# One order of steps in an expert layer: 24 shared steps, all 39 routed tiles in a row, then 20 shared steps

## The chip, the cores and the metric

The kernel runs on one core of a Trainium2 chip. The time is that of one launch on the device, in microseconds (us), median of several runs. The core has TensorE (PE, matrix products; PEld is its weight load), VectorE (DVE), ScalarE (ACT), GpSimd (POOL) and SyncE (SP, which here only starts DMAs), 16 DMA engines, an on-chip memory of 128 partitions, and PSUM banks into which PE writes.

## What is computed

Two layers act on 2048 tokens of 512 features, each an attention-like part and a feed-forward part, each part with layer norm and a residual. The change is in the last part, a mixture of experts:

```python
shared = jnp.einsum('ti,hi->th', jax.nn.silu(x @ sh_gate_w.T) * (x @ sh_up_w.T), sh_down_w)   # I_SH = 1408
probs = softmax(x @ router_weight.T);  top_v, top_i = top_k(probs, 2)                         # 8 experts
for e in range(E):
    gu = x @ gate_up_proj[e].T
    gate, up = (gu[:, :I_MOE], gu[:, I_MOE:])                                                 # I_MOE = 352
    cur = jax.nn.silu(gate) * up @ down_proj[e].T
    out = out + cur * combine[:, e:e + 1]
out = out + jax.nn.sigmoid(x @ shared_gate_w.T) * shared
```

## The kernel before

`build` calls four phases; the last is `experts_phase`. All matrix products are in float32 split in two: every operand has a high part (`_hi`, an ACT copy to a shorter format) and a low part (`_lo`, the difference, made on DVE), and each product is three matmuls (hi·hi, hi·lo, lo·hi).

Each token goes to its two best experts only. POOL scatters the token rows to a DRAM buffer `moe_xs` sorted by expert and padded to tiles of 128 rows; there are always `RT_TILES` = 39 tiles, and the expert that owns a tile is read from the table `owner` at run time.

The work is a list made by `expert_items()`, which each engine walks in the same order, doing its own share of every item:

- **("S", n)**, a shared step, n from 0 to 43: block n // 11 of 512 tokens, chunk n % 11 of 128 hidden columns. PE does gate and up into `moe_ps_g`, `moe_ps_u` (24 matmuls of 512 columns, `shared_gu`) and the down product of step n-1 into the four banks `moe_acc` (12 matmuls, `shared_down`). ACT and DVE split the weights of the next step (`sgu_split`, `sd_split`), DVE multiplies (`s_mul`, tile `moe_hs`), both split the product. It loads 512 KB and 256 KB of weights.
- **("R", i)**, a routed tile. PE does gate and up of tile i (`routed_gu`, 24 matmuls of 352 columns), turns the input of tile i+1 (`turn_xs`), does the down product of tile i-1 (`routed_down`, 9 matmuls) and turns the product of tile i (`turn_h`). ACT and DVE split the weights that come: a "pair" (half of gate and up, 128x1408, `pair_split`) twice, and the down weights (128x1536, `rd_split`), then `xs_split`, `hT_split`, `r_mul` (tile `moe_hr`), `rows`. SP loads 2 x 704 KB and 768 KB of weights into `y`, 256 KB of rows from `moe_xs`, and stores 256 KB of rows to `moe_rows`.
- **("C", m)**, the combine of token tile m: POOL gathers its two rows per token, DVE mixes and takes the statistics (`mix`, `stats`, `shift`), ACT normalises (`norm`), POOL adds the residual. **("F", m)** finishes the last four tiles.

Routed weights have short rings: three pair buffers (the load of pair p waits for the DVE split of pair p-3, `pair_lo`), two down buffers, two input buffers. SP starts its DMAs strictly in the order of its program: in tile n the input of tile n+2, pair 2n+4, the store of tile n-2, the down weights of tile n+1, pair 2n+5. DVE's order in tile n is `hT_split(n-1)`, `rd_split(n-1)`, `pair_split(2n+2)`, `r_mul(n)`, `xs_split(n+1)`, `pair_split(2n+3)`. `turn_h(n)`, the last thing that PE does in a tile, waits for `xs_split(n+1)`.

The list before, in short (`PRE_SHARED` = 12): S0 to S10, the loads of the first tiles (R-1), S11, R0, R1, S12, R2, R3, S13, ..., R36, R37, S30, R38, S31, R39, S32, R40, S33, S34, C0, C1, S35, C2, C3, ..., S39, C10, C11, S40, C12, S41, C13, S42, C14, S43, C15, S44 (the last down product), F12 to F16. R39 and R40 hold only what is left of tiles 38 and 37.

Of the kernel before, what the change touches and what calls it, by code (L numbers as in the profile page):

```python
# [1101 lines left out]
DK = 3  # L1102
LAST = I_MOE - 2 * P
NL = 10
PRE_SHARED = 12
CMB = TPB * (NB - 1)


def expert_items():

    items = [("S", n) for n in range(PRE_SHARED - 1)] + [("R", -1), ("S", PRE_SHARED - 1)]
    n = PRE_SHARED
    for i in range(RT_TILES):
        items.append(("R", i))
        if i % 2:
            items.append(("S", n))
            n += 1
    items += [("S", n), ("R", RT_TILES), ("S", n + 1), ("R", RT_TILES + 1)]
    n += 2
    todo, left = list(range(NT)), N_SH - n  # L1120
    for k in range(left):
        items.append(("S", n + k))
        if k:
            share = -(-len(todo) // (left - k))
            items += [("C", m) for m in todo[:share]]
            todo = todo[share:]
    return items + [("S", N_SH)] + [("F", m) for m in range(CMB, NT)] + [("F", NT)]


def experts_phase(nc, io, keep):  # L1130
# [9 lines left out]
    with ExitStack() as ctx:  # L1140
# [59 lines left out]
        acc = [ps(f"acc{t}") for t in range(TPB)]  # L1200
        io_xs, io_rows = io["moe_xs"], io["moe_rows"]
        items = expert_items()

        def free_gu(eng, k):
# [1150 lines left out]
```

## Time and profile before

| | us |
|---|---|
| median of 3 runs | 2231.64 (2224.86 to 2236.63) |
| the profiled execution | 2235.23 |
| its span, first to last instruction | 2233.5 |
| expert phase, first product of the router to the end | 1515.4 to 2233.5 |
| PE busy | 2008.1 (90%) |
| DVE / ACT / POOL busy | 1478.4 / 1180.8 / 712.8 |
| moved by DMA | 244.97 MB, mean 110 GB/s |

A time line of an engine has, in each row, the start, the duration, the line of the kernel, the tile written and those read, and in square brackets how long the engine had been idle and whose work ended that. Times are from the start of the span. Matmuls overlap, so the step from one start to the next tells PE's pace, not the duration. The "granted clock" (PEclk) is 1.00 at 2.4 GHz and 0.50 at 1.2 GHz.

### The profile page before, as it was taken

Reading aid. Unit: us, or ns where it says so; the run is one execution under the profiler, and the core shown is the slowest. Engines: PE = TensorE matmul, PEld = TensorE weight load, DVE = VectorE, ACT = ScalarE, POOL = GpSimd, SP = SyncE. Lnnn points to the kernel's source line nnn. Section 1 sums busy time; section 2 is a strip of 40 time slices with the busy share of each in tenths; the row PEclk is TensorE's granted clock in tenths of the full one; section 3 lists DMA queues with packets and bytes.
Section 4 is the critical chain, followed back from the end, with each engine's and each line's share of the span. In section 5 each row is a group of like instructions: output and inputs, shape, how many; then the busy total and the mean of one; then the engine's idle time right before and its main releaser. Section 6 shows DMA issues by size and latency. Waiting matters only on the chain. (4 is left out here: it accounts for less than half of the span.)

```text
span 2233.5 us, 32625 instructions
## 1 busy us (share of the span) xinstructions
PE 2008.1 (90%) x10142; PEld 1682.8 (75%) x10142; DVE 1478.4 (66%) x3466; ACT 1180.8 (53%) x2944; POOL 712.8 (32%) x1013
## 2 busy tenths in 40 slices
PE   6885999966999999999999999868689999999976
PEld 4664778744888888888888888757578888888754
DVE  6556655774667767676667677885247777767475
ACT  4663222234666666666666666643246666766332
POOL 0123000143555555555555555640500000000263
PEclk9887999977999999999999999978899999999998
DMA  4143111128000000000000000123568888887463
GB/s 186 43 160 127 42 30 34 38 95 289 16 20 11 20 10 20 10 20 10 20 10 20 10 1 2 62 71 100 209 222 285 298 283 290 293 286 265 144 217 122
DMA packets 78765, 244.97 MB, mean 110 GB/s; under 512 B 9729, under 2 KB 10369, under 8 KB 76577
## 3 DMA queue, kind: packets, MB, share of 16 engines
q1 hardware_dynamic: 73488, 226.46, 29.5%
q0 software_dynamic: 5120, 16.78, 2.2%
q8 instruction: 56, 0.92, 0.2%
q14 instruction: 101, 0.82, 0.1%
HBM read 207.81 MB, written 45.61 MB: 113 GB/s over the span
## 5 line engine op out<-in xcount | busy, mean ns | idle before, releaser
L266 PE MATMUL att_ps_xt<-att_w_hi,xT_hi 128*128 128x512 f32 x512 | 206.2, 403 | 28.3 <-DVE att_w_lo L2021 11.5
L1964 POOL TENSOR_SCALAR att_pr<-att_pr,att_ri 128x384 f32<-128x384 f32 (+2 forms) x256 | 136.5, 546 | 275.2 <-DVE att_ri L2059 275.2
L266 PE MATMUL att_ps_xt<-att_w_lo,xT_hi 128*128 128x512 f32 x512 | 203.8, 398 | 0.0
L266 PE MATMUL att_ps_xt<-att_w_hi,xT_lo 128*128 128x512 f32 x512 | 203.7, 398 | 0.0
L2157 ACT ACTIVATE att_pr<-att_pr,att_nb,att_r 128x384 f32<-128x384 f32 (+2 forms) x256 | 168.0, 659 | 40.0 <-DVE att_nb L2046 39.4
L2102 ACT ACTIVATE att_qkv<-att_ps_xt 128x512 f32<-128x512 f32 x128 | 76.3, 596 | 199.9 <-PE att_ps_xt L266 189.4
L1323 POOL DMA_INDIRECT y<-moe_rows,moe_slotA x16 | 16.3, 1021 | 501.7 <-DMA moe_rows<-moe_lo_f 498.6
L2149 ACT ACTIVATE att_pT_hi<-att_ps_pt 128x768 fp32r<-128x768 f32 (+2 forms) x128 | 93.7, 732 | 121.9 <-PE att_ps_e L266 120.2
L266 PEld LDWEIGHTS att_ps_xt<-att_w_hi,xT_hi 128*128 128x128 f32 x512 | 97.2, 190 | 58.6 <-POOL att_w_lo L1937 22.6
L1969 POOL TENSOR_TENSOR att_rot<-att_rot 128x384 f32<-128x384 f32 x128 | 129.3, 1010 | 21.2 <-DVE att_rot L2012 21.2
L1461 DVE TENSOR_TENSOR moe_rgu_lo<-y,moe_rgu_hi 128x1408 fp32r<-128x1408 f32 x78 | 126.2, 1618 | 5.9 <-ACT moe_rgu_hi L1606 5.9
L2029 DVE TENSOR_TENSOR att_q_lo<-att_ps_xt,att_q_hi 128x256 fp32r<-128x256 f32 x128 | 54.1, 423 | 112.7 <-ACT att_k_hi L2139 112.7
L1606 ACT ACTIVATE moe_rgu_hi<-y 128x1408 fp32r<-128x1408 f32 x78 | 107.7, 1383 | 36.8 <-PE moe_ps_u L1722 22.3
L893 ACT ACTIVATE ffn_sg<-ffn_ps_g,ffn_scale 128x512 f32<-128x512 f32 x44 | 30.2, 687 | 169.1 <-PE ffn_ps_g L266 169.1
L2042 DVE CUSTOM_DVE_ANT_0 att_pr<-att_ps_s,att_mask 128x384 f32<-128x384 f32 (+2 forms) x256 | 118.5, 501 | 1.1 <-issue 1.1
L2003 DVE TENSOR_TENSOR att_rot<-att_qkv,att_tab 128x256 f32<-128x256 f32 x128 | 54.5, 426 | 94.8 <-POOL att_r L1930 94.7
L2220 PE MATMUL att_ps_pt<-ident,att_pr 128*128 128x128 f32 x672 | 96.2, 276 | 23.3 <-POOL att_pr L1964 23.3
L2109 ACT ACTIVATE att_sq<-att_qkv 128x128 f32<-128x128 f32 x384 | 115.2, 317 | 0.3
L266 PEld LDWEIGHTS att_ps_xt<-att_w_hi,xT_lo 128*128 128x128 f32 x512 | 97.2, 190 | 23.9
L266 PEld LDWEIGHTS att_ps_xt<-att_w_lo,xT_hi 128*128 128x128 f32 x512 | 97.3, 190 | 22.8
L1930 POOL TENSOR_TENSOR att_r<-att_ms,att_nhalf 128x3 f32<-128x3 f32 x128 | 110.4, 863 | 10.6
L1452 DVE TENSOR_TENSOR moe_hs<-moe_ps_u,moe_sg 128x512 f32<-128x512 f32 x44 | 30.3, 689 | 123.1 <-issue 112.3
(330 smaller groups left out, 6738.0 us busy)
## 6 DMA issues: line engine op xcount, KB each, us to landing
y<-in_moe_rt SPq DMA_DIRECT2D x78, 704.0 KB, 5.9
y<-in_moe_rt SPq DMA_DIRECT2D x39, 768.0 KB, 5.8
moe_sraw_gu<-in_moe_sgu SPq DMA_DIRECT2D x44, 512.0 KB
moe_sraw_d<-in_moe_sd SPq DMA_DIRECT2D x44, 256.0 KB
moe_xs<-in_zeros SPq DMA_DIRECT2D x39, 256.0 KB
moe_lo_f<-moe_xs SPq DMA_DIRECT2D x39, 256.0 KB, 5.5
moe_rows<-moe_lo_f SPq DMA_DIRECT2D x39, 256.0 KB, 3.5
att_raw_w<-in_qkv_w SPq DMA_DIRECT2D x8, 1024.0 KB, 4.7
```

What stands on the lines that cost most here:

```text
L266: mm = pe.matmul(out, lhsT, rhs, start=(i == 0), stop=(i == len(terms) - 1))
L1461: dve.tensor_tensor(rgu_lo[:, p % 3, :], rraw_gu(p), rgu_hi[:, p % 3, :].bitcast(F32), ALU.subtract) \
L1606: act.activation(rgu_hi[:, p % 3, :], rraw_gu(p), ACT.Copy).then_inc(s("pair_hi"), 1)
L1930: pool.tensor_tensor(r[:, i % 4, :], ms[:], nhalf[:], ALU.pow).then_inc(s("r"), 1)
L1964: pool.tensor_scalar(p, p, ri[:, j % 2, g:g + 1], 1.0, ALU.mult, ALU.mult).then_inc(s("p"), 1)
L1969: pool.tensor_tensor(rot[:, i % 2, :], rot[:, i % 2, :], rot2[:], ALU.add).then_inc(s("roped"), 1)
L2042: dve.tensor_tensor_reduce(pr[:, j % 2, g, WT * P - w:WT * P], ps_s[:, g, 0:w], mask[:, WT * P - w:WT * P], 1.0, -3e38, ALU.add, ALU.max, ...
L2102: act.activation(qkv[:, i % 2, :], ps_x, ACT.Copy).then_inc(s("qkv"), 1)
L2109: act.activation(sq[:, h, :], qkv[:, i % 2, HD * h:HD * (h + 1)], ACT.Square, accum_out=ss[:, h:h + 1]) \
L2149: act.activation(pT_hi[:, 0:w, :, :], ps_pt[:, 0:w, :, :], ACT.Copy).then_inc(s("pT_hi"), 1)
L2157: act.activation(p, p, ACT.Exp, scale=r[:, j % 4, g:g + 1], bias=nb_[:, j % 2, g:g + 1], accum_out=sm[:, j % 2, g:g + 1]).then_inc(s("exp" ...
L2220: mm = pe.transpose(ps_pt[:, u, g, :], pr[:, j % 2, g, P * (WT - w + u):P * (WT - w + u + 1)], ident[:])
```

## The change

`PRE_SHARED` goes from 12 to 24, and the shared step after every second routed tile goes. The list is now S0 to S22, R-1, S23, R0, R1, ..., R38 with nothing between, S24, R39, S25, R40, S26, S27, C0, S28, C1, ..., S42, C15, S43, S44, F12 to F16. No instruction is added or taken away; the line numbers behind the change are lower by 3.

```diff
-PRE_SHARED = 12
+PRE_SHARED = 24
...
     for i in range(RT_TILES):
         items.append(("R", i))
-        if i % 2:
-            items.append(("S", n))
-            n += 1
     items += [("S", n), ("R", RT_TILES), ("S", n + 1), ("R", RT_TILES + 1)]
```

The rule that shares the 16 combines out over the shared steps left (`share = -(-len(todo) // (left - k))`) stands as it was; with 18 steps left in place of 11 it gives one per step in place of two.

SP among the routed tiles, before: behind the second pair of a tile (L1239) come the two loads of a shared step (L1223, L1228), then the next tile's input (L1251), its owner (L1232) and its first pair.

```order
L1239 ISA
L1239 DMA y<-in_moe_rt 128x1408
L1223 DMA moe_sraw_gu<-in_moe_sgu 128x1024
L1228 DMA moe_sraw_d<-in_moe_sd 128x512
L1251 DMA moe_lo_f<-moe_xs 128x512
L1232 TENSOR_LOAD moe_owner
L1232 ISA x2
L1239 ISA
L1239 DMA y<-in_moe_rt 128x1408
L1255 DMA moe_rows<-moe_lo_f 128x512
```

SP at the same place now:

```order
L1236 ISA
L1236 DMA y<-in_moe_rt 128x1408
L1248 DMA moe_lo_f<-moe_xs 128x512
L1229 TENSOR_LOAD moe_owner
L1229 ISA x2
L1236 ISA
L1236 DMA y<-in_moe_rt 128x1408
L1252 DMA moe_rows<-moe_lo_f 128x512
L1242 ISA
```

The shared loads are gone from between the tiles; each tile's loads follow the last tile's at once.

DVE among the routed tiles, before: from the product of a tile (L1484) through the shared step (L1439 to L1456) to the down split of that tile (L1466).

```order
L1484 TENSOR_TENSOR moe_hr<-moe_ps_u,moe_sg 128x352
L1472 TENSOR_TENSOR moe_xsT_lo<-moe_ps_t,moe_xsT_hi 128x512
L1461 TENSOR_TENSOR moe_rgu_lo<-y,moe_rgu_hi 128x1408
L1439 TENSOR_TENSOR moe_sgu_lo<-moe_sraw_gu,moe_sgu_hi 128x1024
L1444 TENSOR_TENSOR moe_sd_lo<-moe_sraw_d,moe_sd_hi 128x512
L1452 TENSOR_TENSOR moe_hs<-moe_ps_u,moe_sg 128x512
L1456 TENSOR_TENSOR moe_hs_lo<-moe_hs,moe_hs_hi 128x512
L1476 TENSOR_TENSOR moe_hT_lo<-moe_ps_t,moe_hT_hi 128x384
L1466 TENSOR_TENSOR moe_rd_lo<-y,moe_rd_hi 128x1536
```

DVE at the same place now:

```order
L1481 TENSOR_TENSOR moe_hr<-moe_ps_u,moe_sg 128x352
L1469 TENSOR_TENSOR moe_xsT_lo<-moe_ps_t,moe_xsT_hi 128x512
L1458 TENSOR_TENSOR moe_rgu_lo<-y,moe_rgu_hi 128x1408
L1473 TENSOR_TENSOR moe_hT_lo<-moe_ps_t,moe_hT_hi 128x384
L1463 TENSOR_TENSOR moe_rd_lo<-y,moe_rd_hi 128x1536
```

The four shared instructions have moved out, to before the first tile or behind the last.

DVE behind the routed tiles, before: the end of one combine (from L1517), a whole second one (L1492 to L1523), and the weights of the next shared step (L1439).

```order
L1517 BN_AGGR moe_mv<-moe_st 128x2
L1519 TENSOR_SCALAR moe_ve<-moe_mv 128x1
L1523 SCALAR_TENSOR_TENSOR moe_sh<-moe_mv,moe_rs 128x1
L1492 SCALAR_TENSOR_TENSOR moe_hi_f<-y,moe_wA,moe_hi_f 128x512
L1495 SCALAR_TENSOR_TENSOR moe_hi_f<-y,moe_wB,moe_hi_f 128x512
L1515 BN_STATS moe_st<-moe_hi_f 128x6
L1517 BN_AGGR moe_mv<-moe_st 128x2
L1519 TENSOR_SCALAR moe_ve<-moe_mv 128x1
L1523 SCALAR_TENSOR_TENSOR moe_sh<-moe_mv,moe_rs 128x1
L1439 TENSOR_TENSOR moe_sgu_lo<-moe_sraw_gu,moe_sgu_hi 128x1024
```

And now, from the end of one shared step (L1453) to the start of the next (L1436):

```order
L1453 TENSOR_TENSOR moe_hs_lo<-moe_hs,moe_hs_hi 128x512
L1489 SCALAR_TENSOR_TENSOR moe_hi_f<-y,moe_wA,moe_hi_f 128x512
L1492 SCALAR_TENSOR_TENSOR moe_hi_f<-y,moe_wB,moe_hi_f 128x512
L1512 BN_STATS moe_st<-moe_hi_f 128x6
L1514 BN_AGGR moe_mv<-moe_st 128x2
L1516 TENSOR_SCALAR moe_ve<-moe_mv 128x1
L1520 SCALAR_TENSOR_TENSOR moe_sh<-moe_mv,moe_rs 128x1
L1436 TENSOR_TENSOR moe_sgu_lo<-moe_sraw_gu,moe_sgu_hi 128x1024
```

One combine stands between two shared steps in place of two.

## Rows read from the trace of the kernel before

**Rows 1.** The page's slices, 55.8 us each: DMA share in tenths.

```profile
DMA  4143111128000000000000000123568888887463
```

**Rows 2.** Stretches: length, busy PE, PEld, DVE, ACT, POOL, clock, DMA share, GB/s.

```profile
1690.46:2061.49 371.03, 371.03 (x1975) 327.52 (x1973) 273.61 (x273) 247.48 (x311) 0.00 (x0) 1.00 0.84 288
```

**Rows 3.** PE's time line: starts of R12, R13, S18 and R14.

```profile
1786.20 0.33 PE L1719 MATMUL moe_ps_g<-moe_rgu_hi,moe_xsT_hi 128*128 128x352 f32 x1
...
1792.82 0.41 PE L1719 MATMUL moe_ps_g<-moe_rgu_hi,moe_xsT_hi 128*128 128x352 f32 x1
...
1799.56 0.48 PE L266 MATMUL moe_ps_g<-xT_hi,moe_sgu_hi 128*128 128x512 f32 x1
...
1808.02 0.33 PE L1719 MATMUL moe_ps_g<-moe_rgu_hi,moe_xsT_hi 128*128 128x352 f32 x1
```

**Rows 4.** PE's time line around R0 and R1, the only two tiles without stock.

```profile
1652.14 0.40 PE L1719 MATMUL moe_ps_g<-moe_rgu_hi,moe_xsT_hi 128*128 128x352 f32 x1 [2.57 <-issue]
...
1666.82 0.41 PE L1744 MATMUL moe_ps_t<-ident,moe_hr 128*128 128x128 f32 x2 [1.77 <-DVE moe_xsT_lo L1472]
...
1667.09 0.48 PE L266 MATMUL moe_ps_g<-xT_hi,moe_sgu_hi 128*128 128x512 f32 x1
```

**Rows 5.** PE's waits from 1640 to 1690 us: total, times, longest.

```profile
PE moe_ps_t L1744 <- DVE moe_xsT_lo L1472: 3.3, 2, 1.8
```

**Rows 6.** PE's time line, shared steps S32, S33, S38, S39 and S43.

```profile
2088.55 0.40 PE L266 MATMUL moe_ps_g<-xT_hi,moe_sgu_hi 128*128 128x512 f32 x1
...
2096.95 0.39 PE L266 MATMUL moe_ps_g<-xT_hi,moe_sgu_hi 128*128 128x512 f32 x1
...
2147.59 0.47 PE L266 MATMUL moe_ps_g<-xT_hi,moe_sgu_hi 128*128 128x512 f32 x1 [2.53 <-DVE moe_hs L1452]
...
2160.29 0.47 PE L266 MATMUL moe_ps_g<-xT_hi,moe_sgu_hi 128*128 128x512 f32 x1 [2.54 <-DVE moe_hs L1452]
...
2205.93 0.39 PE L266 MATMUL moe_ps_g<-xT_hi,moe_sgu_hi 128*128 128x512 f32 x1
```

**Rows 7.** The page's DMA issues: KB each, median us from issue to landing.

```profile
y<-in_moe_rt SPq DMA_DIRECT2D x78, 704.0 KB, 5.9
y<-in_moe_rt SPq DMA_DIRECT2D x39, 768.0 KB, 5.8
...
moe_lo_f<-moe_xs SPq DMA_DIRECT2D x39, 256.0 KB, 5.5
moe_rows<-moe_lo_f SPq DMA_DIRECT2D x39, 256.0 KB, 3.5
```

**Rows 8.** DVE's time line in R13.

```profile
1798.05 0.69 DVE L1472 TENSOR_TENSOR moe_xsT_lo<-moe_ps_t,moe_xsT_hi 128x512 fp32r<-128x512 f32 x1 [0.23 <-ACT moe_xsT_hi L1621]
```

**Rows 9.** Other stretches, columns as in rows 2.

```profile
1642.00:1650.00 8.00, 7.57 (x33) 5.79 (x31) 4.15 (x4) 5.20 (x6) 0.00 (x0) 1.00 1.02 404
1652.14:1667.09 14.95, 11.67 (x72) 10.71 (x72) 10.34 (x11) 10.78 (x12) 0.00 (x0) 1.00 0.97 348
1667.09:1677.09 10.00, 10.00 (x40) 7.98 (x37) 4.76 (x7) 6.39 (x12) 0.00 (x0) 0.83 0.55 192
2122.93:2197.45 74.52, 57.87 (x216) 44.70 (x217) 54.53 (x87) 24.57 (x36) 48.30 (x43) 0.91 0.69 220
```

**Rows 10.** SP's time line in R13, the second pair's issue.

```profile
1797.55 0.33 SPq L1239 DMA_DIRECT2D y<-in_moe_rt  x1
```

**Rows 11.** ACT's time line in R1: it waited for a pair to land.

```profile
1663.73 1.38 ACT L1606 ACTIVATE moe_rgu_hi<-y 128x1408 fp32r<-128x1408 f32 x1 [2.22 <-DMA y<-in_moe_rt]
```

**Rows 12.** DMA issues at 1655.8 us alone, that pair's load: us to landing.

```profile
y<-in_moe_rt SPq DMA_DIRECT2D x1, 704.0 KB, 7.9
```

**Rows 13.** PE's waits from 2113 to 2198 us.

```profile
PE moe_ps_g L266 <- DVE moe_hs L1452: 17.3, 7, 4.1
```

**Rows 14.** DVE's time line in the tail, the start of two combines in a row.

```profile
2113.19 0.75 DVE L1492 SCALAR_TENSOR_TENSOR moe_hi_f<-y,moe_wA,moe_hi_f 128x512 f32<-128x512 f32 x1
...
2115.78 0.75 DVE L1492 SCALAR_TENSOR_TENSOR moe_hi_f<-y,moe_wA,moe_hi_f 128x512 f32<-128x512 f32 x1
```

## The prediction

> **What bounds the kernel now.** I read the slices of the page first: in the expert phase, the last third, the DMA share is 8 tenths while the routed tiles run, far above most of the kernel [rows 1]. Then the table of stretches. From S13 to S30, 17 periods of one shared step and two routed tiles, PE is busy all 371.03 us at the full clock, and DMA has a share of 0.84 [rows 2]. So PE is the bound there, with DMA not far behind. Third, PE's time line: a period is 1808.02 - 1786.20 = 21.82 us, of which R12 has 6.62, R13 6.74 and the shared step 8.46 [rows 3]. A routed tile costs PE 6.68 us on average. Fourth, the two places where PE does wait: at the first tiles, 2.57 us before R0 and 3.3 us inside R0 and R1 [rows 4, 5]; and in the tail, where shared steps go with two combines each: S38 to S39 takes 12.70 us, against 8.40 from S32 to S33 [rows 6].
>
> **What the mix did for the DMA.** A routed tile moves 2 x 704 + 768 + 256 + 256 = 2688 KB, that is 2.75 MB [rows 7]; a shared step 0.79 MB. A period moves 6.29 MB in 21.82 us, 288 GB/s, as the row says [rows 2]. Alone, a routed tile at PE's pace wants 2.75 MB / 6.68 us = 412 GB/s. The shared steps gave 8.46 us of PE work in which the queue caught up and ACT and DVE had room. They leave; that is the cost of the change. The gains lie at both ends.
>
> **Part 1, the routed stretch (cost).** 39 tiles in a row. The first two find their loads landed, so 36 steps from one tile's start to the next (R2 to R38) run at a pace T that I have to bound. PE alone gives 6.68. DVE and ACT do not raise it: in R13, which already follows another tile, DVE waited only 0.23 us for ACT before the input split and made the pace of 6.74 us [rows 3, 8].
>
> By throughput: with loads alone in flight the DMA moved 404 GB/s over 8 us [rows 9], which gives 2.75 / 0.404 = 6.8 us. In R0 and R1, the only back-to-back tiles without stock, it moved 348 GB/s at a share of 0.97 [rows 9], with stores and reads mixed as they will be: 7.9 us. If the engine time per byte were that of the mixed stretch (0.84 of 21.82 is 18.3 us a period; a shared step's 0.79 MB at 348 GB/s takes 2.3 of it), a tile would take 8.0.
>
> By the loop of the ring: in a tile that starts at P, SP issues the load of the second pair when DVE has split a first pair, at P + 4.7 (1797.55 against the start 1792.82) [rows 3, 10]; where DVE is held by a late landing, as described next, 5.0. When a pair lands late, ACT waits for it, splits it, and only then does the silu and the input's split, for which `turn_h` waits: landing at about 1663.7, the next PE step at 1667.09, 3.4 us [rows 4, 11]. That next step is two tiles on, so T = (5.0 + 3.4 + L) / 2, with L the time to landing. L = 5.9, the median of all pairs [rows 7], gives 7.15; L = 7.9, as in R1 with a queue ahead [rows 12], gives 8.15.
>
> So T lies between 6.8 and 8.15. I take 7.7: nearest to the R0 and R1 rows (7.9), a little less, since those two tiles also shared the queue with the 0.79 MB of a shared step, and the median L says less. Cost: 36 x (7.7 - 6.68) = 36.7 us.
>
> DMA: Bandwidth & Descriptors of the Trainium skill, section Bandwidth, says that for transfers between HBM and on-chip memory the HBM side binds at about 358 GB/s a core, and elsewhere in that section that one core alone reached 425. By 358 a tile would take 7.7 us, and the change would cost what I take. The 404 GB/s of the trace is above 358, so that figure is no ceiling here; the trace stands between the two.
>
> **Part 2, the start (gain).** SP's loads of the first tiles stand between S22 and S23 in place of S10 and S11. There they waited for the up product of S10, since block 0 had to be done with its buffer; now this was long ago, so they start some 4 us earlier, and shared loads ahead are few. The waits of 2.57 and 3.3 us go [rows 4, 5], and so does what the clock lost behind them: 0.83 over 10 us, a mean of stretches at 2.4 and at 1.2 GHz [rows 9]: S12 took 10.00 us in place of 8.46. Gain 5.9 + 1.5 = 7.4.
>
> **Part 3, the tail (gain).** S32 to S43, 11 steps, takes 2205.93 - 2088.55 = 117.4 us; at 8.40 each it would be 92.4 [rows 6]. Of the 25.0 between, 17.3 is PE waiting for DVE's product [rows 13], the rest mostly the lower clock that follows it, 0.91 over the stretch [rows 9]. With one combine a step DVE has half as much to do between two shared steps. From one combine's mixing to the next, DVE takes 2115.78 - 2113.19 = 2.59 us [rows 14]; the step of 12.70 holds two and a PE wait of 2.54 [rows 6]. One of them off, and with it one ACT copy that stands ahead of the weights, that wait is just covered, and without a wait the clock has no cause to fall. So I take a step with one combine as hidden under 8.40 and the gain as 25.0, which is also its most; what hides a combine is PE's own 8.40, with little to spare. If the step only lost what it sheds (12.70 - 2.59 - 0.7 = 9.4), 12 such steps would give 12 back and the gain would be 13. The seven shared steps that join the tail cost 8.40 in place of 8.46: with the others, 19 x 0.06 = 1.1 gained. SP's loads for S24 and S25 now go out ahead of R0 and lie in their buffer through the stretch, so the tail finds them; PE's wait for the last tile's down product in S31 moves to S24 unchanged. POOL's gathers are one per step too, and the last gathers start as before, two shared steps behind the last tile. ACT's output of block 2 (four copies) now falls in a step with a combine: 0.5 lost.
>
> **Sum.** 36.7 - 7.4 - 25.0 - 1.1 + 0.5 = +3.7 us on the profiled execution's 2235.2, so 2238.9. That execution is 3.6 above the median of the three runs, so on the scale of the median the sum comes to 2235.3; as I can't say which of the two the kernel after will fall on, I give 2237, between them. The point of no change is T = 6.68 + 33.0 / 36 = 7.60.
>
> **Rivals.**
>
> *The DMA holds its full rate.* If the stretch runs as at 1642 to 1650 us (404 GB/s [rows 9]), T is 6.8 to 7.2 and the cost 4 to 19 us: at 7.0 the sum is 11.5 - 33.0 = -21.5, 2210. For: a steady queue of three or four loads hides each load's start. Against: R0 and R1 had such a queue and moved 348. By the fit that the Trainium skill gives in DMA: Bandwidth & Descriptors, section Anatomy of one DMA (2.0 us and the bytes at 436 GB/s, fitted on POOL's path), a pair would land in 3.7 us and nothing would be lost at all; the rows have 5.9.
>
> *The ring's latency decides, slower.* One mechanism: with no shared step to drain the queue, each second pair stands behind a pair, a store and the down weights, L stays at 7.9 as in R1 [rows 12], T is 8.15 and the cost 52.9: +19.9, 2252. PE then idles 1.5 us a tile; in R1 an idle of 1.77 us was followed by a stretch at 1.2 GHz [rows 4, 9], which took 1.5 us; once in six tiles that would add 9. It is slower than before from T = 7.60 on, and beyond 0.5% from T = 7.9. For: the 348 GB/s too. Against: the median of 5.9 in the mixed stretch, half of whose pairs are second ones.
>
> *The tail keeps its wait.* If a single combine still makes DVE late, the gain is 13 in place of 25 and all else as forecast: +15.7, 2248.
>
> *Nothing changes in the order.* The order of the built program shows that it does, so no chance for this.
>
> **Chances.** Forecast (T from 7.3 to 7.9) 0.50; full rate 0.14; ring's latency 0.30; tail 0.06. The range leaves out the outer part of the full rate and the clock's extra: 2216 to 2257. The measurement can tell about 0.5%, 11 us, from no change: below 2220.5 lies T under 7.3, above 2242.8 lies T over 7.9, or the tail. Faster 0.16, same 0.48, slower 0.36.
>
> **What the profile after would show.** The starts of the routed tiles on PE's time line: a steady 7.7 us, with about 1 us idle each, put down to the input's low part on DVE and behind it to ACT waiting for a pair. DMA share over the stretch at 0.95 or more and 350 to 370 GB/s. No wait before R0. Shared steps at 8.4 in the tail, no wait for `moe_hs`, clock 1.00. A tile pace of 7.0 or 8.2, or PE waiting in the tail, would make this wrong; a low clock in the routed stretch would be a term that I left out.

## The result, and the profile after

| | median us | ratio to before | 95% interval |
|---|---|---|---|
| before, 8 runs | 2230.61 | 1 | |
| after, 8 runs | 2250.49 | 1.0098 | 1.0078 to 1.0118 |

The changed kernel is slower by 20 us, 1.0%: more than the 0.5% that this kernel's measurement can tell from no change, and inside the predicted range of 2216 to 2257. The likeliest case, no change to tell, did not come. The time lies next to the rival of the ring's latency (2252), to which the prediction gave 0.30, but by luck: that rival had T = 8.15 and the tail's whole gain of 25, and what came is a T nearer to the forecast's own and a tail that gained 15.

The profiled executions are 2235.23 and 2251.17. In both, PE waits once in S6, long before the first change in the order, for 17.29 us before and 11.46 after. It has nothing to do with the change (it is absent in eight of the runs below), so I count from the steps behind it: from the start of S11 to the end the kernel before takes 592.5 us and the one after 615.2, **22.6 more**, where the prediction has 3.7.

PE's time line after, four starts: S22, R0, R2, R38. The number in brackets is PE's idle time ahead.

```profile
1726.50 0.40 PE L266 MATMUL moe_ps_g<-xT_hi,moe_sgu_hi 128*128 128x512 f32 x1
...
1744.67 0.40 PE L1716 MATMUL moe_ps_g<-moe_rgu_hi,moe_xsT_hi 128*128 128x352 f32 x1 [0.79 <-issue]
1750.69 0.41 PE L1741 MATMUL moe_ps_t<-ident,moe_hr 128*128 128x128 f32 x2 [1.50 <-DVE moe_xsT_lo L1469]
...
1758.00 0.40 PE L1716 MATMUL moe_ps_g<-moe_rgu_hi,moe_xsT_hi 128*128 128x352 f32 x1
...
2042.31 0.40 PE L1716 MATMUL moe_ps_g<-moe_rgu_hi,moe_xsT_hi 128*128 128x352 f32 x1
```

R2 to R38 is 284.31 us for 36 tiles: T = **7.90** us, in place of the 7.7 forecast and of PE's 6.68 [rows 3]. The stretch as a row (columns as in rows 2), and who waited in it (total, times, longest):

```profile
1758.00:2042.31 284.31, 252.03 (x1444) 226.60 (x1441) 230.04 (x217) 210.83 (x253) 0.00 (x0) 0.98 0.95 347
```

```profile
SPq L1229 <- DVE moe_rgu_lo L1458: 105.4, 35, 4.4
SPq L1236 <- DVE moe_rgu_lo L1458: 34.8, 35, 1.1
SPq L1242 <- DVE moe_rd_lo L1463: 22.7, 36, 1.6
```

```profile
ACT moe_rgu_hi L1603 <- DMA y<-in_moe_rt: 65.9, 35, 2.9
PE moe_ps_t L1741 <- DVE moe_xsT_lo L1469: 32.0, 30, 2.3
```

The row of the stretch answers rows 2 and 9: PE no longer busy throughout, DMA share 0.95, 347 GB/s, just what R0 and R1 had moved. The SP rows are the ones I had not made enough of: in nearly every tile SP waits 3 us for DVE's split of a pair before it may start the next one (L1229 reads the tile's owner, in front of the first pair). The last two rows are the sign that the prediction named: PE idle for 0.9 us a tile ahead of `turn_h`, for the input's low part on DVE, and behind that ACT waiting for a pair to land.

The tail, two of the waits from 2110 to 2222 us (ACT's for its weights, PE's for `moe_hs`) and two starts, S33 and S42 (S32 starts at 2119.70):

```profile
ACT moe_sgu_hi L1573 <- DMA moe_sraw_gu<-in_moe_sgu: 8.4, 6, 2.1
PE moe_ps_g L266 <- DVE moe_hs L1449: 7.2, 5, 2.1
```

```profile
2130.15 0.47 PE L266 MATMUL moe_ps_g<-xT_hi,moe_sgu_hi 128*128 128x512 f32 x1 [1.91 <-DVE moe_hs L1449]
...
2213.48 0.39 PE L266 MATMUL moe_ps_g<-xT_hi,moe_sgu_hi 128*128 128x512 f32 x1
```

Ten steps in 93.8 us, where ten times 8.39 is 83.9: 9.9 us lost. That is less than the 25 of before [rows 6, 13], but not nothing, as forecast.

### The profile page after: what moved, and what is told of

Read it like the earlier page. It is cut to its first block and busy times, and to the rows that moved or that the text cites. A ratio compares the mean times of both kernels' runs of the same rounds, so it can differ in the third digit from the quotient of the medians.

```text
span 2249.4 us, 32625 instructions
## 1 busy us (share of the span) xinstructions
PE 2008.4 (89%) x10142; PEld 1677.5 (75%) x10142; DVE 1471.0 (65%) x3466; ACT 1182.3 (53%) x2944; POOL 710.9 (32%) x1013
## 5 line engine op out<-in xcount | busy, mean ns | idle before, releaser
L266 PEld LDWEIGHTS att_ps_xt<-att_w_hi,xT_hi 128*128 128x128 f32 x512 | 96.7, 189 | 59.7 <-POOL att_w_lo L1934 22.6
L266 PE MATMUL att_ps_o<-att_o_hi,att_e_hi 128*128 128x512 f32 x256 | 103.1, 403 | 6.7 <-POOL att_o_lo L1938 4.7
```

What stands on the lines that cost most here:

```text
L266: mm = pe.matmul(out, lhsT, rhs, start=(i == 0), stop=(i == len(terms) - 1))
```

## What paces the routed stretch

Two readings fit the row. Either the DMA is full at 347 GB/s (its share says 0.95), or the ring of three buffers starts its loads too late. In slices of 0.6 us, from 1850 to 1874 us:

```profile
DMA  9899999999968989999999998498798899999959
GB/s 347 343 376 399 423 440 412 421 414 371 252 192 279 360 352 394 365 428 409 402 428 419 359 246 148 165 323 327 308 382 343 353 412 431 412 387 378 306 197 359
```

Three times in 24 us, once a tile, the rate falls from over 400 to 150 to 250 GB/s and stays under 380 for some 2 us more, while the busy share falls in one slice of each dip alone (to 6, 4 and 5 tenths) and shows 7 to 9 in the slices around it, some of which moved only 148 to 279 GB/s. So the share is no proof of a full pipe. In the records of the single packets, 5632 bytes took 215 ns while the queue was fed and up to 670 ns, as a mean over half a microsecond, in a dip, and all of that counts as busy. That an engine waits there for the first bytes of a load that was started late is my reading of it. What stands there on SP, ACT and DVE:

```profile
1862.91 0.33 SPq L1236 DMA_DIRECT2D y<-in_moe_rt  x1
1863.28 0.43 SPq L1252 DMA_DIRECT2D moe_rows<-moe_lo_f  x1
1864.48 0.90 SPq L1242 DMA_DIRECT2D y<-in_moe_rt  x1
1866.02 0.33 SPq L1236 DMA_DIRECT2D y<-in_moe_rt  x1
1866.40 0.63 SPq L1248 DMA_DIRECT2D moe_lo_f<-moe_xs  x1
1870.65 0.33 SPq L1236 DMA_DIRECT2D y<-in_moe_rt  x1
...
1878.75 0.33 SPq L1236 DMA_DIRECT2D y<-in_moe_rt  x1
```

```profile
1873.56 1.38 ACT L1603 ACTIVATE moe_rgu_hi<-y 128x1408 fp32r<-128x1408 f32 x1 [2.21 <-DMA y<-in_moe_rt]
```

```profile
1875.32 0.52 DVE L1481 TENSOR_TENSOR moe_hr<-moe_ps_u,moe_sg 128x352 f32<-128x352 f32 x1 [1.72 <-ACT moe_sg L1614]
1875.81 0.69 DVE L1469 TENSOR_TENSOR moe_xsT_lo<-moe_ps_t,moe_xsT_hi 128x512 fp32r<-128x512 f32 x1
1876.41 1.61 DVE L1458 TENSOR_TENSOR moe_rgu_lo<-y,moe_rgu_hi 128x1408 fp32r<-128x1408 f32 x1
```

This closes a loop over two tiles: a tile's first pair starts at 1862.91, its second 3.11 later (1866.02); that lands 7.5 us after, ACT takes it at once (1873.56), DVE splits it behind `moe_hr` and `moe_xsT_lo` (to 1878.02), and SP, behind the read of the owner, starts the first pair of the tile two on at 1878.75. The medians over the stretch are 3.11, 7.42 and 5.22, and (3.11 + 7.42 + 5.22) / 2 = **7.88**. That is the loop of the prediction's rival, (5.0 + 3.4 + L) / 2, cut at other places, with L = 7.4 in place of 7.9. The sum alone does not tell a late issue from a full pipe, since a full pipe would lengthen L too; the experiments do.

## The experiments

"Before" in this section is the kernel before on the same chip. The runs come from three chips, on which the median of the kernel before was 2215.5, 2214.6 and 2227.7 us, while the expectations give their times on the scale of the result (2230.6 before, 2250 after); so it is the ratios and T that have to be compared. T is from R2 to R38 in the profiled execution.

| run | edit to | ratio to before | interval | T us | GB/s there |
|---|---|---|---|---|---|
| after, again | | 1.0094 | 1.0061 to 1.0127 | 7.91 | |
| 31 shared steps ahead | after | 1.0164 | 1.0149 to 1.0180 | 7.96 | 345 |
| late store | after | 1.0063 | 1.0049 to 1.0077 | 7.83 | 349 |
| fourth pair buffer | after | 1.0042 | 1.0027 to 1.0057 | 7.49 | 365 |
| short down load | after | 1.0044 | 1.0029 to 1.0060 | 7.48 | 331 |
| SP's order | after | 1.0045 | 1.0019 to 1.0071 | 7.53 | 364 |
| buffer, order, late store | after | 0.9863 | 0.9846 to 0.9879 | 6.71 | 406 |
| the same and output behind the split | after | 0.9848 | 0.9823 to 0.9873 | 6.71 | |
| the same and first loads earlier | after | 0.9859 | 0.9816 to 0.9902 | 6.71 | |
| a shared step after each third tile | before | 1.0015 | 1.0004 to 1.0025 | | |
| late store | before | 0.9980 | 0.9971 to 0.9990 | | |
| third tile, late store, output | before | 0.9953 | 0.9937 to 0.9970 | | |

### The kernel after, again

> The kernel after once more, beside the others and the kernel before. Expected 1.0098 of the kernel before, some 22 us; it gives the step from which the single edits are counted.

As expected, with a wide interval. Its loop has the same medians, 3.11, 7.44 and 5.22.

### Stretch and tail apart

```diff
-PRE_SHARED = 24
+PRE_SHARED = 31
```

> The kernel after with 31 shared steps ahead of the routed tiles and 13 behind, so that the tail has two combines a step again, as before. It tells the cost of the stretch from the gain of the tail. If the books of the trace hold (R2 to R38 at 7.90 us a tile in place of 6.68, 43.9 lost; some 5 won at the start; the tail as before), it runs 38 us longer than the kernel before, at 2269, and the tail's PE waits for the product on DVE (moe_hs) are back at about 17 us in 7 waits. Rival: the tail won little with one combine a step (it kept its own waits), and the time stays at that of the kernel after, 2250.

1.0164 of 2215.5 us is 36 us more than before, close to the 38 expected, and 14 to 15 more than the kernel after (1.0098): so the tail with one combine a step does bring some 15 us, and the stretch with the start costs some 36. PE's wait of before is back (from 2135 to 2220 us: total, times, longest):

```profile
PE moe_ps_g L266 <- DVE moe_hs L1449: 17.6, 7, 4.1
```

### The tail: SP's wait for a store

```diff
 # SP, at combine n
-                    if 1 <= n <= CMB:
-                        store_x(n - 1)
-                    if TPB <= n + 2 < NT and n >= 2:
-                        load_x(n + 2)
+                    if 2 <= n <= CMB + 1:
+                        store_x(n - 2)
+                    if TPB <= n + 1 < NT:
+                        load_x(n + 1)
```

> The kernel after, with SP's program alone changed in the tail: at combine m it stores the result of combine m-2 in place of m-1 (long finished, so SP does not wait) and loads the residual rows of tile m+1 in place of m+2; the next shared weights stand behind these. Theory: the shared steps of the tail that took 10.5 us (every other one) did so since SP waited for POOL's addition of combine m-1, which stands behind two gathers, before it could start the next shared load; then their waits go, ACT no longer waits for sraw_gu, and 5 to 8 us are won: 2243 to 2246. Rival: one combine is still too much work for DVE (my third rival): then the waits for moe_hs stay at 7 us and the time at 2250.

In the kernel after, POOL's addition of combine m-1 stands behind the two gathers of combine m+4, the store waits for it, and the next shared load stands behind the store. POOL's time line, then SP's, then ACT's:

```profile
2115.70 0.98 POOL L1320 DMA_INDIRECT y<-moe_rows,moe_slotA  x1 [0.18 <-issue]
2116.99 1.85 POOL L1320 DMA_INDIRECT y<-moe_rows,moe_slotB  x1 [0.30 <-issue]
2118.87 1.30 POOL L1331 TENSOR_TENSOR y<-y,moe_hi_f 128x512 f32<-128x512 f32 x1
```

```profile
2120.20 0.34 SPq L1261 DMA_DIRECT2D out<-y  x1
2120.58 0.52 SPq L1257 DMA_DIRECT2D y<-x_mid  x1
2121.15 0.46 SPq L1220 DMA_DIRECT2D moe_sraw_gu<-in_moe_sgu  x1
```

```profile
2125.40 1.06 ACT L1573 ACTIVATE moe_sgu_hi<-moe_sraw_gu 128x1024 fp32r<-128x1024 f32 x1 [1.17 <-DMA moe_sraw_gu<-in_moe_sgu]
```

With the late store PE's wait from S32 to S42 is:

```profile
PE moe_ps_g L266 <- DVE moe_hs L1449: 0.7, 1, 0.7
```

S32 to S42 takes 84.9 us in place of 93.8. In time it gave 1.0098 - 1.0063 (two chips), 7.8 us, and in the two profiled executions 8.9 us in the tail and 2.2 in the stretch, which the edit does not touch and where T varies (7.90 to 7.96 in the three runs with the same stretch and without this edit): the theory holds, the rival (one combine too much for DVE) falls. What is left, 0.7 us in one step, is ACT's output of block 2 ahead of the split; it goes with the last edit of this section.

### Is the pipe full?

```diff
 # fourth raw buffer: the low part of block 1's input, no longer read by then
-        rraw_gu = lambda p: yf[:, PAIR * (p % 3):PAIR * (p % 3 + 1)]
+        rraw_gu = lambda p: lo_f[:, :, BLK:BLK + PAIR // KD] if p % 4 == 3 \
+            else fold(yf[:, PAIR * (p % 4):PAIR * (p % 4 + 1)])
...
-                if p >= 3:
-                    sp.wait_ge(s("pair_lo"), p - 2)
+                if p >= 4:
+                    sp.wait_ge(s("pair_lo"), p - 3)
```

> The kernel after, with a fourth buffer for the raw routed pairs (in the low part of the block 1 input, free by then), so that SP may start the load of pair p when pair p-4 is split, in place of p-3. Bytes and order stay. Theory throughput: the DMA is full at about 347 GB/s, so a tile stays at 7.8 to 7.9 us, the time to landing grows by about what the loads start earlier, and the time stays within 4 us of 2250. Rival, the latency of the ring: loads start 2 us or more earlier and land earlier, a tile takes about 7.0 us, the time is 2218.

```diff
-                sp.dma_start(rraw_d(i), io["moe_rt"][owner_of(i), :, 2 * PAIR:2 * PAIR + DK * D]
+                sp.dma_start(rraw_d(i)[:, 0:2 * D], io["moe_rt"][owner_of(i), :, 2 * PAIR:2 * PAIR + 2 * D]
```

> The kernel after, with 512 KB of down weights loaded for each routed tile in place of 768 (the third chunk is left out, its buffer keeps old data; all splits and products are still made). A tile then moves 2.49 MB in place of 2.75. Theory throughput: at 347 GB/s a tile takes 7.17 us, 36 x 0.73 = 26 us less: 2224. Rival, latency of the ring, (5.0 + 3.4 + L) / 2: only L falls, by the 0.75 us that the shorter load ahead takes, a tile takes 7.5 us and the time is 2236.

Both say that 347 GB/s is no ceiling. With the same bytes and a fourth buffer the core moved 365 GB/s and T fell to 7.49. With a tenth of the bytes gone T fell to 7.48, not to 7.17, and the rate fell too, to 331: the value expected by the loop was 7.5, and its medians are 3.11 + 6.70 + 5.22 = 15.03, half of it 7.5. But the fourth buffer alone fell short of its rival's 7.0 as well. SP's waits in it show what came next, the store of rows, which waits for ACT and stands ahead of the down weights and the second pair:

```profile
SPq L1254 <- ACT moe_lo_f L1630: 94.9, 36, 6.5
SPq L1244 <- DVE moe_rd_lo L1465: 58.4, 36, 1.6
```

### SP's order in the tile

```diff
                     if n + 2 < RT_TILES:
                         load_xs(n + 2)
                         load_pair(2 * n + 4)
-                    if n >= 2:
-                        store_rows(n - 2)
-                    if n + 1 < RT_TILES:
-                        load_rd(n + 1)
                     if n + 2 < RT_TILES:
                         load_pair(2 * n + 5)
+                    if n + 1 < RT_TILES:
+                        load_rd(n + 1)
+                    if n >= 2:
+                        store_rows(n - 2)
```

> The kernel after with SP's order in the routed tile changed alone (second pair ahead of the down weights, the store of rows last); three pair buffers as before, the old store in the tail. The loop read from the trace of the kernel after: first pair's issue to the second pair's 3.11 us, its landing 7.42 later, from there 5.22 to the issue of the first pair two tiles on; 15.75 for two tiles, 7.88 each. Theory: the second pair no longer stands behind 768 KB of down weights, lands 1.5 to 1.9 us sooner, the loop is 13.9 to 14.3 and a tile 7.0 to 7.1 us: 28 us less than the kernel after, 7 under the kernel before. Rival: SP waits for DVE's split of the pair three back anyway, the order alone changes nothing, 7.9 us a tile.

The order alone won 0.37 us a tile, less than half of what I expected: the second pair lands 6.55 us after its issue, 0.9 sooner and not 1.5 to 1.9, and the loop is (3.06 + 6.55 + 5.31) / 2 = 7.46. The rival, no change, falls too; as the first pair now lands later (7.3 us after its issue in place of 6.2), the bytes in front were, it seems, spread anew rather than gone.

Fourth buffer, SP's order and late store together, each edit as shown above:

> The kernel after, with the fourth pair buffer, the late store of the tail, and in each tile SP's order changed: input of tile n+2, pair 2n+4, pair 2n+5, down weights of n+1, and only then the store of tile n-2, which waits for ACT (2.6 us a tile in the run with the fourth buffer alone). Bytes stay. In the traces so far the DMA moves 410 to 425 GB/s while SP has loads queued and drops to some 150 GB/s for 2 us in each tile, where SP waits and starts nothing. Theory, the gap in the issues alone sets the pace: with no gap a tile takes 6.7 to 6.9 us, 32 us less than in the late-store run: 18 to 24 us under the kernel before (ratio 0.990). Rival, a ceiling of the DMA for this mix, reached at the 367 GB/s of the fourth buffer: the pace stays at 7.4 to 7.5 and the time is within 5 us of the kernel before.

Both together, with the late store, is **0.9863** of before, 30 us less, where I had expected 18 to 24. The tiles account for it: 36 x (7.83 - 6.71) = 40 us against the run with the late store alone, where I had counted 32. The stretch as a row, and the rate in slices of 0.6 us from 1850 to 1874, to be laid beside that of the kernel after:

```profile
1745.45:1986.89 241.44, 241.44 (x1443) 224.61 (x1441) 231.02 (x217) 210.15 (x252) 0.00 (x0) 1.00 1.02 406
```

```profile
GB/s 365 422 372 377 421 430 387 393 441 408 438 421 432 422 409 418 434 379 399 434 402 438 411 383 406 387 442 422 410 389 410 446 445 412 376 441 429 366 374 419
```

PE is busy all 241.44 us; every tile takes 6.71. The dips to 150 GB/s are gone, and so are the long packets: between 1850 and 1874 us 99 of 100 packets of 5632 bytes took 224 ns or less. So 39 tiles in a row can run at PE's pace at 406 GB/s: the ring was the limit, not the pipe. Perfetto Trace Analysis of the Trainium skill, section Engine Utilization under Roofline, says that a core alone on its memory can pull more than its share of 358 GB/s, up to about 435; the 406 agrees with that. The same page's section Optimization Strategy says that a gap which keeps coming back can mean too few buffers; here that was one of two causes, the order of issue being the other: each edit alone won about 0.4 us a tile, both together 1.2.

```diff
 # ACT, in a shared step
-                    if n % SH_CHUNKS == 1 and n > 1:
-                        shared_out(n // SH_CHUNKS - 1)
                     if n + 1 < N_SH:
                         sgu_split(n + 1)
                     sd_split(n)
+                    if n % SH_CHUNKS == 1 and n > 1:
+                        shared_out(n // SH_CHUNKS - 1)
```

> The run with fourth buffer, SP order and late store, and in addition ACT's output of a finished block (four copies, 2.4 us) moved behind the split of the next shared weights. Theory: the step in the tail that took 9.2 us for it takes 8.4, the step of the second output likewise: 1 to 2 us less than that run, 0.9858 of the kernel before. Rival: the down product of the next block waits for the output instead, and the time is the same or 1 us more.

0.9848, on another chip than the run before it; the intervals overlap, so the time alone shows nothing. The steps do: S34 takes 8.42 us in place of 9.23, and S23 8.48 in place of 9.70 (though S23 varied from 8.74 to 9.78 in runs without this edit), with no idle time of PE left ahead of R0. This is the fastest version of the study together with the one before it, 1.4 to 1.5% under the kernel before.

```diff
-    items = [("S", n) for n in range(PRE_SHARED - 1)] + [("R", -1), ("S", PRE_SHARED - 1)]
+    items = [("S", n) for n in range(PRE_SHARED - 2)] + [("R", -1)] + [("S", PRE_SHARED - 2), ("S", PRE_SHARED - 1)]
...
-                    sp.wait_ge(s("s_up"), SH_CHUNKS)
+                    sp.wait_ge(s("s_up"), 2 * SH_CHUNKS)
```

> As the run with everything, and the loads of the first routed tiles one shared step earlier (behind S21, when block 1 is done with its input). Theory: the first pairs have landed when ACT comes to them, the wait of 1.1 us ahead of R0 goes: 1 to 1.5 us less than the run with everything, 0.9852. Rival: ACT and DVE split the first pairs a step earlier and a shared step waits for that instead; no gain.

The rival, and in the trace worse (from S11 to the end 566.5 us, where the run before has 561.3; the medians, 0.9859 and 0.9848, can't be told apart). The theory had lost its ground in the run before, where PE no longer waited ahead of R0. Now ACT waits 5.21 us for the first pair to land, with the next shared weights behind it, and PE waits 3.29 us for `moe_hs` ahead of S23. ACT's time line in S22:

```profile
1736.82 1.38 ACT L1605 ACTIVATE moe_rgu_hi<-y 128x1408 fp32r<-128x1408 f32 x1 [5.21 <-DMA y<-in_moe_rt]
```

### The other way: less of the mix

```diff
-        if i % 2:
+        if i % 3 == 2:
             items.append(("S", n))
```

> The kernel before, with one shared step after every third routed tile in place of every second: 13 in the stretch, and 6 more in the tail, where each then has one combine. SP's program is the old one. Theory: three tiles and a shared step (9.04 MB in 28.5 us, 317 GB/s) are still bounded by PE, R at 6.7 and S at 8.5, and the tail loses 10 us in place of 25, as in the kernel after: 15 us under the kernel before (0.993). Rival: three tiles in a row already fall into the loop of the ring, the third one at 7.9: 13 x 1.2 = 16 us lost again and the time that of the kernel before.

The rival: 0.15% slower than before. Three tiles and a shared step need 317 GB/s, well under what the DMA can do, yet the third tile falls into the loop. PE's time line at the end of R20, a third tile that started at 1829.91, and the start of the shared step:

```profile
1838.68 0.66 PE L1744 MATMUL moe_ps_t<-ident,moe_hr 128*128 128x128 f32 x2 [2.14 <-DVE moe_xsT_lo L1472]
1839.13 0.42 PE L1745 MATMUL moe_ps_t<-ident,moe_hr 128*96 128x128 f32 x1
1839.20 0.78 PE L266 MATMUL moe_ps_g<-xT_hi,moe_sgu_hi 128*128 128x512 f32 x1
```

The first two tiles behind a shared step take 6.6 and 6.7 to 6.8 us, the third 7.5 to 9.3. The demand averaged over a period did not tell that the ring would be late within it.

The kernel before with the late store, the edit shown above, and nothing else:

> The kernel before, with the late store of the tail alone (two combines a step stay). Theory, DVE's two combines bound the step of 12.70 us: less than 3 us are won. Rival, SP's late start of the shared load bounds it, as it did with one combine: 10 to 20 us under the kernel before.

PE's waits from 2091 to 2172 us:

```profile
PE moe_ps_g L266 <- DVE moe_hs L1452: 16.1, 6, 4.1
```

0.9980, 4 to 5 us; in the profiled execution the steps with two combines stay at 12.70 and only S41 is shorter, by 3. So in the tail of before the two combines set the step, and SP's store did not; it became the bound when the change took one away.

The third-tile edit with the late store and the output behind the split, as shown above:

> One shared step after every third tile, the late store, and ACT's output of a finished block moved behind the split of the next shared weights. Theory: every step of the tail but the first takes 8.4 us, so the whole 25 us of the tail are won: 25 us under the kernel before (0.989). Rival, as for the third-tile run: the stretch gives 16 of it back and it is 9 under (0.996).

0.9953: the third tile's loss and the tail's gain, as its rival had it. In this run every step from S26 to S42 takes 8.37 to 8.45 us, so with both edits the tail has nothing left to give.

Not run was the kernel before with the fourth buffer and the new order of SP, its tail mended as here. So the 1.4 to 1.5% are what the new order of steps gives together with these edits; they do not show that leaving the mix is better than keeping it with a mended ring.

## Why the prediction was right in range and wrong in its likeliest case

- **What bounds before, and the sign of each part.** Right: the stretch lost, start and tail gained.
- **The routed pace.** Forecast 7.7, measured 7.90: 36 x 0.20 = 7.1 us more. The two bounds were set side by side and the value taken between them: throughput gave 7.9 by R0 and R1, and a little was taken off for the shared step's bytes in their queue and because "the median L says less". The loop was the true one of the two, and its L was 7.4, between the 5.9 of the mixed stretch and the 7.9 of R1 [rows 7, 12]. The step that failed is to have pulled L down to 7.0, which is what 7.7 means in the loop, by a median taken where shared steps empty the queue. The 348 GB/s of R0 and R1, my ground for 7.9, is no rate that the pipe is bound to, and it was misread: "with stores and reads mixed as they will be" is not so, since SP's time line of before shows loads alone from 1651.85 to 1663.38 us, no store. The 347 of the stretch follows from the loop's T and agrees with it by chance.
- **The rival "full rate".** Its ground (404 GB/s in rows 9) was sound: the pipe does 406. It did not come since SP did not ask for it in time.
- **The clock in the stretch.** The forecast put it at nothing, and named a low clock as a term left out. Three times PE ran at half speed for 3.4 us, behind idle times of 2.0 to 2.3 us. One of the three as a row of stretches:

```profile
1797.77:1801.18 3.41, 3.41 (x14) 3.41 (x13) 3.41 (x4) 2.27 (x4) 0.00 (x0) 0.50 0.90 282
```

  Little can be left to add for it: the loop alone gives 7.88 of the 7.90. That a PE which is not the bound makes up for a slow stretch out of its next idle time fits this, but no run shows it by itself.
- **The start.** Forecast a gain of 7.4, measured 4.6 from S11 on (5.1 with the 0.5 that S10 lost): S10 to R2 lost 6.8 us before, S22 to R2 loses 1.7 after. Other executions of the same two lists (before with the late store; after, again) lost 4.7 and 2.5, so the gain is 2 to 5. Of "the waits of 2.57 and 3.3 us go", 1.50 us of the second stands in R0 in every run, since R0 has no down product to cover the input's split; and 0.79 is left ahead of R0. That last one has a cause that the prediction left out: ACT's output of block 1 (2.4 us) now falls in S23, ahead of the split of the next shared weights. In the two runs without it in the step ahead of R0 (31 shared steps ahead; the output behind the split) that step takes 8.47 and 8.48 us in place of 9.43, and PE does not wait. The clock's part (1.5) came as forecast.
- **The tail.** Forecast a gain of 25.0, measured some 15: 9.9 us lost in ten steps. The step that failed is "what hides a combine is PE's own 8.40": it weighed DVE's work and one ACT copy, but not SP's queue, in which the next shared load stands behind a store that waits for POOL. It is the third rival's size by another mechanism; its own (DVE late with a single combine) was refuted by the late store.
- **The sum.** 7.1 for the pace, 2.8 for the start and 9.4 for the tail (9.9 less the 0.5 that was in the sum), less 0.4 since the shared steps moved gained 1.5 in place of 1.1, is 18.9 over the forecast; 3.7 + 18.9 = 22.6, as in the trace. Of the signs named as proof, the share of 0.95 came, and so did the 0.9 us of PE's idle time a tile, for DVE's low part; the 350 to 370 GB/s was 347, a steady pace did not come (single tiles take 6.7 to 9.2 us), and the tail had the wait for `moe_hs`.

## What to carry to other kernels

For a ring of buffers write down the loop (issue, landing, what the consumer does before it lets go, next issue) and divide by the tiles it spans; compare that with PE's pace before asking for the bandwidth, and take the landing time from where the queue will be as full. A DMA share near 1 with a rate that dips in fine slices can be a late issue and not a full pipe, as here. On an issuing engine that works in order, put what has to wait for another engine (stores) behind what the next step needs, and count that queue wherever a step gets shorter.

## What the runs showed of the hardware

- One core moved 406 GB/s over 241 us, a tenth of it stores, where 347 had looked full at a share of 0.95. Between 1856 and 1873 us of the kernel after, a packet of 5632 bytes took 215 ns while the queue was fed and, as a mean over half a microsecond, 380 to 670 ns in the dips; all of it counts as busy.
- The wait in S6 (17.29 us before, 11.46 after) falls while POOL scatters the rows. It goes with the place of the run and not with the edit: the six profiled executions taken beside medians of 2230.6 and 2227.7 us for the kernel before all have it (9 to 17 us), and the eight beside 2215.5 and 2214.6 us have none. Why, the runs don't show.
